# Cross-attention over a 32-batch add: ten halved slots, weights in 8 KB pieces, 17 warm-up transposes, 13 row reloads

## What is computed

```python
# x, ctx_1024: (32, 512, 512) f32; Wq, Wk, Wv: (512, 512) f32; 16 heads of 32
q = (tgt @ Wq.T).reshape(B, N, NH, dk).transpose(0, 2, 1, 3)
k = (memory @ Wk.T).reshape(B, N, NH, dk).transpose(0, 2, 1, 3)
v = (memory @ Wv.T).reshape(B, N, NH, dk).transpose(0, 2, 1, 3)
scores = jnp.einsum('bhqd,bhkd->bhqk', q, k) * scale
probs = jax.nn.softmax(scores, axis=-1)
att = jnp.einsum('bhqk,bhkd->bhqd', probs, v)
att = att.transpose(0, 2, 1, 3).reshape(B, N, D)
tgt2 = att[0]
return tgt + tgt2
```

## Time and profile before

| | |
|---|---|
| runs | 186.4, 186.23, 185.81 us; median 186.23 |
| profiled execution | 185.45 us; its span from first to last instruction 183.6 us |
| busy | PE 132.1, DVE 102.4, ACT 97.2, POOL 77.8 us |
| DMA | 71.52 MB, 390 GB/s mean over the span |
| mean granted clock of TensorE | 0.893 of full speed |

### The profile page before, as it was taken

How to read it: one execution, slowest core, us unless ns; L and a number is a source line. 1 busy time by engine, 2 the same in 40 slices (tenths; PEclk the granted TensorE clock), 3 DMA queues, 4 the chain that set the end, 5 groups by cost and what they waited for, 6 DMA issues and landing times.

```text
span 183.6 us, 3367 instructions
## 1 busy us (share of the span) xinstructions
PE 132.1 (72%) x1240; PEld 92.4 (50%) x1240; DVE 102.4 (56%) x163; ACT 97.2 (53%) x225; POOL 77.8 (42%) x41
## 2 busy tenths in 40 slices
PE   6999999999989998998987998899887000000000
PEld 6878858677656675556765556566565000000000
DVE  0444135634759399934499677685541999920000
ACT  2525526468668469867898668797974000000000
POOL 1000000000039299600039999259995899910000
PEclk9999999999999999999999999999999755555555
DMA  6999999999999998999999999999999999999998
GB/s 211 361 378 417 408 411 411 409 411 406 409 409 401 384 370 298 370 397 400 408 403 405 393 355 397 403 408 408 403 416 405 387 406 407 384 401 404 409 407 320
DMA packets 31168, 71.52 MB, mean 390 GB/s; under 512 B 1840, under 2 KB 7984, under 8 KB 31024
## 3 DMA queue, kind: packets, MB, share of 16 engines
q1 hardware_dynamic: 31152, 71.31, 101.1%
HBM read 37.75 MB, written 33.55 MB: 388 GB/s over the span
## 4 chain that ended last, share of the span: by engine, by line
PE 55%; DVE 13%; ACT 12%; issue 6%; DVEq 1%; POOL 0%; ACTq 0%; POOLq 0%
PE bank L439 13%; PE bank L417 8%; PE bank L373 7%; PE bank L450 7%; PE bank L393 6%; ACT probs L647 6%; PE bank L404 6%; DVE slots L784 5%; ACT probs_t L656 4%; PE bank L364 4%; DVE neg_max L728 3%; DVE slots L774 3%; PE bank L529 2%; PE bank L626 1%; DVEq L68 1%
## 5 line engine op out<-in xcount | busy, mean ns | idle before, releaser
L319 POOL TENSOR_TENSOR slots<-slots,att_rows 128x512 f32<-128x512 f32 (+1 forms) x23 | 40.5, 1794 | 73.9 <-DVE att_rows L754 73.9
L728 DVE TENSOR_REDUCE neg_max<-bank 128x1 f32<-128x512 f32 x64 | 41.6, 682 | 19.1 <-PE bank L417 18.8
L647 ACT ACTIVATE probs<-bank,neg_max 128x512 f32<-128x512 f32 x64 | 44.6, 698 | 10.8 <-DVE neg_max L728 10.3
L439 PE MATMUL bank<-ident,probs 128*128 128x128 f32 x256 | 40.7, 283 | 6.2 <-ACT probs L647 5.8
L656 ACT COPY probs_t<-bank 128x512 f32<-128x512 f32 x62 | 36.4, 590 | 12.5 <-PE bank L439 8.3
L439 PEld LDWEIGHTS bank<-ident,probs 128*128 128x128 f32 x256 | 27.8, 140 | 24.5 <-ACT probs L647 17.7
L417 PE MATMUL bank<-k_t,q_t 32*128 32x512 f32 x192 | 24.4, 426 | 0.1
L328 POOL TENSOR_TENSOR slots<-slots,att_rows 128x1024 f32<-128x1024 f32 x8 | 18.6, 2370 | 5.6 <-DVE att_rows L754 5.6
L336 POOL TENSOR_TENSOR slots<-slots,att_rows 128x2048 f32<-128x2048 f32 x4 | 18.0, 4532 | 3.0 <-DVE att_rows L754 3.0
L767 DVE TENSOR_TENSOR slots<-slots,bank 128x512 f32<-128x512 f32 (+1 forms) x21 | 18.5, 906 | 0.0
L450 PE MATMUL bank<-probs_t,v 128*32 128x128 f32 x496 | 17.3, 276 | 1.5 <-ACT probs_t L656 1.4
(11 more groups left out here) (46 smaller groups left out, 95.6 us busy)
## 6 DMA issues: line engine op xcount, KB each, us to landing
slots<-in_x_dram SPq DMA_DIRECT2D x18, 1024.0 KB, 17.3
slots<-in_x_dram SPq DMA_DIRECT2D x28, 512.0 KB, 9.4
out_dram<-slots SPq DMA_DIRECT2D x28, 512.0 KB, 9.4
out_dram<-slots SPq DMA_DIRECT2D x12, 1024.0 KB, 12.3
out_dram<-slots SPq DMA_DIRECT2D x24, 256.0 KB, 6.4
ctx_raw<-in_ctx_dram SPq DMA_DIRECT2D x1, 1024.0 KB, 4.9
wq_raw<-in_L_xattn_Wq_dram SPq DMA_DIRECT2D x1, 1024.0 KB, 9.2
wv_raw<-in_L_xattn_Wv_dram SPq DMA_DIRECT2D x1, 1024.0 KB, 12.1
```

Source lines behind the costliest of these rows:

```text
L319: nc.gpsimd.tensor_tensor(xs, xs, a.unsqueeze(1).to_broadcast([P, BPS, a.shape[1]]), ALU.add).then_inc(added[g], 1)
L439: last = nc.tensor.transpose(bank[:, PT_BANK + h % 2, t * P:(t + 1) * P], probs[:, h % 2, t * P:(t + 1) * P], ident[:, :])
L647: nc.scalar.activation(probs[:, h % 2, :], bank[:, h % S_BANKS, :], ACT.Exp, bias=neg_max[:, h:h + 1], scale=1.0, accum_out=row_sum[:, h:h ...
L728: nc.vector.tensor_reduce(neg_max[:, h:h + 1], bank[:, h % S_BANKS, :], AX_X, ALU.max, negate=True).then_inc(max_ready, 1)
```

## The change

The diff (comments and blank lines left out). `wq_t[:, :, i::T]` is every fourth column, from i.

```diff
-    WARM_UP, KEEP_UP = 24, 16
+    WARM_UP, KEEP_UP = 17, 16

-    HALVED = range(12)
-    POOL_HALVED, DVE_HALVED = (1, 3, 5, 7, 9, 11), (0, 2, 4, 6, 8, 10)
-    POOL_WHOLE, DVE_WHOLE = (13, 15), (12, 14)
+    HALVED = range(10)
+    POOL_HALVED, DVE_HALVED = (1, 3, 5, 7, 9), (0, 2, 4, 6, 8)
+    POOL_WHOLE, DVE_WHOLE = (11, 13, 15), (10, 12, 14)

-    BY_ROWS = range(FRESH, FRESH + 12)
+    BY_ROWS = range(FRESH, FRESH + 13)

-    FIRST_ORDER = (1, 3, 0, 5, 2, 4, 7, 6, 8, 9, 10, 11)
-    SECOND_ORDER = (1, 3, 0, 5, 2, 7, 9, 4, 11, 6, 8, 10, 13, 12, 15, 14)
+    FIRST_ORDER = (1, 3, 0, 5, 2, 4, 7, 6, 8, 9)
+    SECOND_ORDER = (1, 3, 0, 5, 2, 7, 9, 4, 6, 8, 11, 10, 12, 13, 15, 14)

             if what == "wq_t":
-                return wq_t[:, :, i * P:(i + 1) * P]
+                return wq_t[:, :, i::T]
             if what == "wk_t":
                 return wk_t[:, :, half, i * P:(i + 1) * P]
-            return {"ctx_t": ctx_t, "wv_t": wv_t, "k_t": k_t}[what][:, i, half, :]
+            if what == "wv_t":
+                return wv_t[:, i, half, :].rearrange("p (n t) -> p t n", t=T)
+            return {"ctx_t": ctx_t, "k_t": k_t}[what][:, i, half, :]

-            wq_rows = wq.rearrange("(t p) d -> p t d", p=P)
-            sp.dma_start(wq_raw[:, :, :], wq_rows).then_inc(wq_loaded, 16)
+            sp.dma_start(wq_raw[:, :, :], wq.rearrange("(p t) d -> p t d", p=P)).then_inc(wq_loaded, 16)
-            sp.dma_start(wv_raw[:, :, :], wv.rearrange("(t p) d -> p t d", p=P)).then_inc(wv_loaded, 16)
+            sp.dma_start(wv_raw[:, :, :], wv.rearrange("(p t) d -> p t d", p=P)).then_inc(wv_loaded, 16)
```

## The result

The changed kernel takes **187.08 us** at the median (186.62 to 190.34, 8 runs), the kernel before 186.15; the ratio is **1.0055, 95% interval 1.0035 to 1.0074**: slower by about 1.0 us. Ratios leave out the slow executions, those over 1.5% above their kernel's fastest: here the one of 190.34 us, two of e6, one of e12 and one of the kernel before. The profiled execution spans 185.2 us (before 183.6).

What follows compares the result with a forecast made beforehand. The DMA queue was taken to bound the kernel; at 145 us its date moved -0.9 + 1.21 = +0.31, less 0.25 us it was early = +0.06, so 186.23 + 0.06 = 186.3 us. Range 185.3 to 187.2.

Steps and rivals of the forecast that it cites:

- The weights' new order: Copies into wq_t and wv_t written with a step of four elements: taken to cost nothing, with 0.3 us of slack.
- Rival 3: Strided writes cost double: TensorE waits 2.2 us at the value matmuls near 32 us, end at 188.5; chance 0.06.
- The warm-up: Seventeen transposes instead of 24 at the start: compute chain 0.2 us earlier, bounds 0 and -0.22.
- The 0.22 us that I had going: First key matmul's wait for the context's residue, expected to vanish with key weights evacuated before the context arrives.
- The pause ahead of the context: TensorE idle 0.8 us before the context lands at 6.13 us: should not cost the full clock.
- Ten halves: Ten halved groups instead of twelve: first reload issued 0.9 us sooner, 1.21 us more store work behind the 72 us hole.
- the hole at 145 us: Small DMA gap where ROW_3's adds release the final stores, 0.25 us; predicted to close.
- no longer binds: Compute chain's date at 145 us, 0.2 us earlier, would no longer set the end; the DMA queue's would.
- VectorE's side: VectorE's adds under ten halved groups, one halved first add less (0.68 us): counted as no term.
- Rival 2: The hole at 72 us only grows: reload still issued at 70.5 us, +0.96 us, end at 187.2; chance 0.20.
- 8 KB pieces: Query and value weight loads at the start: 0.3 us gained for both, worth nothing at the end by itself.
- Thirteen reloads: Group 14 fetched as 2 x 512 KB instead of 1 MB: 0, moving nothing past 145 us.

Runs made afterwards that it cites:

- e6: The changed kernel with both weights in 2 KB pieces and plain copies again; ratio to the kernel before 0.9979, 185.73 us.
- e12: The kernel before with 12 warm-up transposes instead of 24, nothing else; ratio 1.0015, 186.58 us.
- e2: The kernel before with both weights in 8 KB pieces and copies written with a step of four elements; ratio 1.0077, 187.73 us.
- e7: The kernel before with both weights in 8 KB pieces, copies reading the bank with a step of 128 elements and writing one run; ratio 0.9998, 186.06 us.
- e1: The kernel before with 17 warm-up transposes instead of 24, nothing else; ratio 0.9983, 185.81 us.
- e5: The changed kernel with 24 warm-up transposes again; ratio to the kernel before 1.0081, 187.92 us.
- e10: The kernel before with 17 transposes and 8 KB pieces read with a step, still twelve halves and twelve reloads; ratio 0.9982, 185.59 us.
- e9: The changed kernel in full, but copies read the bank with a step and write one run; ratio to the kernel before 0.9958, 185.44 us.
- e8: The kernel before with ten halved groups and still twelve row reloads; ratio 1.001, 186.44 us.
- e3: The kernel before with ten halved groups and thirteen row reloads, warm-up and weights as before; ratio 1.0008, 186.41 us.
- e4: The kernel before with thirteen row reloads and groups 12 and 13 swapped in the second half's order; ratio 1.0007, 186.29 us.
- e11: The kernel before with Wq alone in 8 KB pieces and written with a step of four, Wv as before; ratio 0.9996, 186.23 us.

## Why the prediction was right or wrong

The measured time lies in the range (185.3 to 187.2), but my likeliest case, no change at 186.3, was not what came: it is slower, for a reason to which I gave 0.06 and which I left out of the range. That the time falls inside is luck: the same mechanism at my price would have given 188.5.

- **The weights' new order** is the step that failed: "I cost it at nothing" should have read +1.2 us. e2 (1.0077) and e6 (0.9979) show it from both sides, and e7, with the same pieces and the same order in SBUF, shows that nothing but the step on the SBUF side makes it (0.9998). I took the bare rows of one-run copies as the nearest, and noted that the cover was 0.3 us thin. The rule that I had cited spoke against that: the Trainium skill (SBUF — State Buffer, section Door 1: The DMA port swizzle, its note on cachelines) says that each access which crosses to a new 16-byte line pays a penalty. Here the trace agrees with it: 0.59 to 1.09 us and 0.69 to 1.08 us for 512 elements. Rival 3 had the mechanism, with its price too high: 2.2 us of waiting for measured 1.2. Copies cost 0.5 more, not 0.6, the residue 0.4 and not 0.7, and ScalarE's idle time took some of it.
- **Rival 3's path** was right in one half. The fourth residue ends at 33.4, and the value matmuls that need it start 0.46 us later than the pace of 0.23 us between matmuls would have had them (the profile shows 0.29 of this as idle). The third residue holds them up by 0.15, and getting back into pace takes the rest of the 0.77. But before that the value matmuls start 0.42 late, counted from K. They write the bank of wv_t's second block, whose residue (the changed kernel's timeline of VectorE, below) ends at 29.50 + 1.10 = 30.6. I had not looked at who frees their bank.

```profile
29.50 1.10 DVE L725 TENSOR_TENSOR wv_t<-bank,wv_t 128x512 fp32r<-128x512 f32 x1 [1.14 <-ACT wv_t L643]
```

- **The warm-up**, "-0.2", had the wrong frame: I read one execution, in which the clock was full at 4.50 us, as the kernel's. The full clock was first recorded between 4.24 and 7.63 us with 24 transposes. With 17 the chain is the same where it comes early and gains 1.06 us where it comes at 7.63. Over many runs that is 0.9983 (e1) and, from e5 to the changed kernel, 1.0081 to 1.0055, neither clear of noise. The 0.22 us that I had going did not go with an early clock: the wait for the context's residue was 0.18 in e1, though VectorE stood idle for 0.82 us ahead of that residue. It waited for ScalarE's copy of the context, not for the key weights.
- **The pause ahead of the context** was called safe, by the earlier trace rows. At the end of the program that holds. At the start, with 12 transposes one profile has the clock at 10.2 us, and with 17 one (e6) lost it for 3.4 us, after an idle time of 2.33 us that a late landing made and not the shorter warm-up alone. Executions with a mean clock of 0.890 or less, as that one, are 7 of 56 with 17 transposes (two of the changed kernel, three of e6, two of e10, none of e1 and e9), 4 of 175 with 24 (one of the kernel before, two of e2, one of e8) and 1 of 12 with 12. They took 187.2 to 190.3 us. So the shorter warm-up may have a price that the ratios show in part only, as these leave out three of the seven. Whether the pause makes these executions or merely the late landing is open: only one was traced.
- **Ten halves** had two terms, -0.9 and +1.21. Neither is in the end. The first came out near its bound of 0, "if SP's issues stay slow for another reason": SP's second issue of the second half took 1.22 us in the changed kernel and 1.39 in e3, and 0.37 in e9. From the second half's normalization to the first reload the traces have 5.9 to 8.1 us over all kernels, with 6.81 before and 6.64 after. In e9 it is 6.04, most of the predicted gain, but the end does not follow it: last - S is 38.12, and the hole at 145 us is there as before (315 GB/s). At the last gate, where ROW_3 releases the final stores, the queue is behind the compute chain by 0.4 us at most (last - S from 38.1 to 38.5). So the compute chain, of which I said that it "no longer binds", sets the date to within 0.4 us in every run. VectorE's side, "no term", is one: 0.14 us of R - F, gained between the normalizations of SECOND and ROW_1 (30.43 us before, 30.28 after), where VectorE's adds changed.
- **Rival 2** gives nearly the measured time (187.2), and the larger hole of the changed kernel looks like its proof. It is not: e3 and e8 carry the same moved stores and end at 1.0008 and 1.001, and e9 carries them and is faster than the kernel before.
- **8 KB pieces** gained more at the start than I took: Wq and Wv land 2.49 us after their predecessors, 2.77 and 2.73 before, 0.5 us in all against 0.3. As predicted it is worth nothing at the end (e7).
- **Thirteen reloads**: 0, as predicted (e4).

## What to carry to other kernels

A DMA queue that looks full from end to end can still be paced by the compute chain at its gates: lay out the dates of the gates, and compare distances between them over several kernels before blaming the largest hole. If data must change its order on the way from PSUM to SBUF, read with the step and write one run. A profile is one draw of when TensorE's clock comes up: judge a warm-up by many executions. Here 17 transposes, which end before the data land even at half clock, gained over 24 where the clock came late; 12 gained nothing over all executions (1.0015), and what 17 cost in rare long executions is not settled.

## What was not expected of the hardware

ScalarE and VectorE read a PSUM bank with a step of 128 fp32 elements at the full rate (0.59 and 0.69 us for 512 elements), while a step of four on the SBUF side costs 0.5 us more on ScalarE (its write) and 0.4 on VectorE (its write and one of its reads). The full clock came at 4.24 to 7.63 us after the same 24 transposes. And a slow stretch between 105 and 111 us is there in four of seven profiles with twelve halves and twelve reloads, and in none of seven with a larger stock in the queue. Over the slowest 2.5 us its packets are slow at a full share in three (311 GB/s before, 361 in e7, 348 in e10); in e2 the share falls too (287 GB/s at 0.93). That points to the stock, but e1, e11 and e12 have the smaller stock and no such stretch, so chance is not ruled out.
